# A fused attention kernel: the product for k, its sums of squares and GpSimd's norms one turn sooner

## The reference

```python
q, k, v = x @ Wq, x @ Wk, x @ Wv            # 16 heads of 64
k, v = concat([mem_k, k]), concat([mem_v, v])  # 4 memory rows
q, k = l2norm(q), l2norm(k)                 # per head
dots = einsum('bhid,bhjd->bhij', q, k) * 10
dots = einsum('hg,bgij->bhij', W_pre_th, dots)   # mixes the heads
dots = where(causal, -max, dots)
dots = where(dots < 64th largest of the row, -max, dots)
attn = einsum('hg,bgij->bhij', W_post_th, softmax(dots))
out = (attn @ v) * head_scale * sigmoid(x @ Wg + bg)
return out @ Wo
```

## Time and profile before

| | us |
|---|---|
| median of 3 runs | 2355.67 (2355.18 to 2355.76) |
| the profiled execution | 2356.68 |
| its span, first to last instruction | 2354.8 |
| TensorE busy in it | 2106.7 |
| VectorE busy in it | 1803.1 |
| ScalarE busy in it | 1608.3 |
| GpSimd busy in it | 822.6 |

### The profile page before, as it was taken

How to read it: one execution, slowest core, us unless ns; L and a number is a source line. 1 busy time by engine, 2 the same in 40 slices (tenths; PEclk the granted TensorE clock), 3 DMA queues, 4 the chain that set the end, 5 groups by cost and what they waited for, 6 DMA issues and landing times. The chain is left out here.

```text
span 2354.8 us, 55179 instructions
## 1 busy us (share of the span) xinstructions
PE 2106.7 (89%) x16059; PEld 1369.2 (58%) x16060; DVE 1803.1 (77%) x7282; ACT 1608.3 (68%) x4676; POOL 822.6 (35%) x2274
## 2 busy tenths in 40 slices
PE   7995699999999999999999999999899889985997
PEld 3433456666666666666666666666666666663433
DVE  6565389968996899689958995899589959993446
ACT  4442578857885788688858885888688758861543
POOL 3001444444444443444344434443443344311000
PEclk9996799999999999999999999999999999987998
DMA  5002012111211121012101211121012101212002
GB/s 175 0 0 85 22 40 61 43 25 43 61 43 26 43 61 43 25 43 61 43 25 43 61 43 25 43 61 43 26 43 61 43 23 41 58 38 87 1 0 72
DMA packets 113217, 104.69 MB, mean 44 GB/s; under 512 B 34449, under 2 KB 110865, under 8 KB 112913
## 3 DMA queue, kind: packets, MB, share of 16 engines
q1 hardware_dynamic: 108000, 96.65, 16.1%
q10 hardware_dynamic: 4912, 4.46, 0.6%
HBM read 19.14 MB, written 12.71 MB: 14 GB/s over the span
## 5 line engine op out<-in xcount | busy, mean ns | idle before, releaser
L1052 PE MATMUL bankC<-R,E 128*128 128x128 f32 x2560 | 351.7, 287 | 40.0 <-POOL R L1403 39.9
L1052 PEld LDWEIGHTS bankC<-R,E 128*128 128x128 f32 x2560 | 338.5, 202 | 76.3 <-POOL R L1403 43.9
L1036 PE MATMUL bankB<-raw,mixpre 128*128 128x76 f32 (+37 forms) x1024 | 353.9, 433 | 19.7 <-DMA raw<-SC 19.4
L1252 ACT ACTIVATE S<-bankB,aim_first 128x68 f32<-128x68 f32 (+56 forms) x456 | 232.3, 513 | 163.7 <-PE bankB L1036 163.3
L1499 DVE TENSOR_SCALAR_CACHE_REDUCE S<-S,minus_thr 128x68 f32<-128x68 f32 (+56 forms) x456 | 218.5, 515 | 139.4 <-POOL minus_thr L1396 137.8
L1387 POOL TENSOR_TENSOR S<-S,diagmask 128x8 f32<-128x8 f32 x512 | 106.8, 213 | 522.5 <-ACT S L1252 484.5
L1403 POOL TENSOR_SCALAR R<-mixpost,rinv 128x128 f32<-128x128 f32 x512 | 184.3, 372 | 284.9 <-DVE rinv L1563 284.5
L1559 DVE SCALAR_TENSOR_TENSOR E<-S,limit,E 128x68 f32<-128x68 f32 (+56 forms) x456 | 221.3, 521 | 35.1 <-ACT E L1278 5.2
L1278 ACT ACTIVATE E<-S,nmax 128x12 f32<-128x12 f32 (+56 forms) x512 | 240.0, 528 | 0.7 <-POOL nmax L1417 0.7
L1078 PEld LDWEIGHTS bankM<-PT,V 128*64 128x64 f32 x5120 | 179.0, 138 | 101.4 <-issue 90.9
L1036 PEld LDWEIGHTS bankB<-raw,mixpre 128*128 128x128 f32 x1024 | 159.7, 192 | 120.4 <-issue 82.5
(11 more groups left out here) (177 smaller groups left out, 3935.4 us busy)
## 6 DMA issues: line engine op xcount, KB each, us to landing
X_first<-in_L_attn_x_dram ACTq DMA_DIRECT2D x8, 512.0 KB, 10.4
x<-X_first SPq DMA_DIRECT2D x8, 512.0 KB, 2.9
xt<-x SPq DMA_DIRECT2D x32, 128.0 KB, 2.4
x<-xt SPq DMA_DIRECT2D x32, 128.0 KB, 2.5
X_last<-x SPq DMA_DIRECT2D x8, 512.0 KB, 6.6
out_dram<-X_last SPq DMA_DIRECT2D x8, 512.0 KB, 2.8
raw<-SC SPq DMA_DIRECT2D x8, 258.0 KB, 2.9
raw<-SC SPq DMA_DIRECT2D x8, 254.0 KB, 3.1
```

The costliest lines, as they stand in the source:

```text
L1036: last = nc.tensor.matmul(bankB[n % 2][:, 0:wide(n)], W.mixpre[:, :], raw[n % RAWS][:, 0:wide(n)], start=True, stop=True)
L1052: last = nc.tensor.matmul(bankC[n % 2][:, jb * P:(jb + 1) * P], E[n % EBUFS][:, jb * P:(jb + 1) * P], R[n % RBUFS][:, :], start=True, stop ...
L1252: nc.scalar.activation(S[n % SBUFS][:, 0:wide(n)], src, ACT.Identity, bias=W.aim_first[:, group(n)]).then_inc(S_out, 1)
```

## The change

The product for k, ScalarE's squares and copies of it, stand at g = 2 instead of g = 4, in the second place. Score quarter 1 takes the first place of g = 4, quarter 2 the second. The product for v of tile 1 moves from g = 2 to g = 4. GpSimd's norm of q stands at g = 2 (before: 4), that of k at g = 4 (before: 6). VectorE's sums of k stand at g = 0 (before: 2), in its own count of turns. The list `uses` follows.

```diff
-V1_AT = 2
+V1_AT = 4
...
                 if g == 2:
                     uses += score_steps(2 * t + 1, 0)
+                if g == 2 and ahead:
+                    uses += two("k", t + 1)
+                if g == 4:
+                    uses += score_steps(2 * t + 1, 1)
+                if early_values(t, g):
+                    uses += two("v", t)
                 if g == 4:
                     uses += score_steps(2 * t + 1, 2)
-                if early_values(t, g):
-                    uses += two("v", t)
-                if g == 2:
-                    uses += score_steps(2 * t + 1, 1)
-                if g == 4 and ahead:
-                    uses += two("k", t + 1)
...
                     if g == 4:
-                        score(2 * t + 1, 2)
+                        score(2 * t + 1, 1)
...
-                    if g == 2:
-                        score(2 * t + 1, 1)
-                    if g == 4 and ahead:
+                    if g == 2 and ahead:
                         tokens(t + 1, "k", Wk)
+                    if g == 4:
+                        score(2 * t + 1, 2)
...
-                    if g == 2:
-                        score(2 * t + 1, 1)
-                    if g == 4 and ahead:
+                    if g == 2 and ahead:
                         project_qk(t + 1, 1, "k")
+                    if g == 4:
+                        score(2 * t + 1, 2)
...
                     if g == 2:
                         copy_halo(t + 1)
+                        norm(t + 1, 0)
                     if g == 4:
-                        norm(t + 1, 0)
-                    if g == 6:
                         norm(t + 1, 1)
...
-                if g == 2 and t and t + 1 < NT:
+                if g == 0 and t and t + 1 < NT:
                     squares(t + 1, 1)
```

## The result

The changed kernel takes 2326.05 us (2323.36 to 2327.89), the kernel before beside it 2355.43 us: a ratio of 0.9873 (0.9861 to 0.9884), 29.4 us less where 34.7 were forecast. The profiled span is 2323.6 us, 31.2 less than before.

The account below looks back on a forecast made before the run. Each sequence was taken as bound by TensorE from the R wait to mid tile 1, then by VectorE. Seven sequences at 3.3 us (23) plus 12 in the first gave 35 us: 2321 us, range 2310 to 2332.

Parts of the forecast that it names:

- The wait of kT: TensorE's waits for the transposes of k, 1.12, 2.19 and 1.89 us in tiles 0, 1 and 2, would go.
- The new wait: Tile 0, sequences 2 to 8: ScalarE's k squares wait for VectorE's q sums; TensorE waits 2.3 us, plus 1.4 of clock.
- Clock in tile 1: Slow matmuls behind tile 1's 2.19 us wait cost 1.7 us more; 1.5 us taken as coming back on average.
- Tile 0: Sequences 2 to 8: 1.1 + 0.7 - 2.3 - 1.4 = -1.9 us, a loss.
- Tiles 2 and 3: Tile 2 gains, of 1.9 us, only the 1.5 that VectorE has to give; tile 3 gains 0.
- What TensorE saves beyond that makes the R wait longer (4.2 to about 4.7).: Tile 3: TensorE's further savings only lengthen its R wait at the start of a sequence.
- The move of v: Product for v of tile 1 only changes places with waits: cost 0, bounds 0.5 us either way for a tile.
- The first sequence: k transposes end at about 273.5 instead of 280.5, 7 us; tiles 1 and 2 add 2.2 + 1.7 + 1.4; together 12.
- The sum: 3.3 us a sequence, seven times, 23 us, and 12 in the first sequence: 35 us, predicting 2321 us.
- Covered: Rival: k squares find q sums ready, so ScalarE's new wait is covered; 61 us gain, 2295 us; chance 0.07.
- VectorE bound from tile 1 on: Rival: TensorE's gain comes back as a longer R wait; no change, 2355 us; chance 0.07.
- GpSimd starves VectorE: Rival: thresholds of g = 4 come late behind the q norm in tiles 2 and 3; 2379 us; chance 0.08.

Follow-up runs that it names:

- e1_two_sq: Changed kernel with a squares buffer of its own for k and 5 instead of 6 E buffers: 2290.83 us.
- e9_before_two_sq: Kernel before with a squares buffer of its own for k and five E buffers in place of six: 2343.24 us.
- e12_before_e5: Kernel before with five E buffers in place of six and nothing else: 2345.33 us.
- e2_e5: Changed kernel with 5 instead of 6 E buffers alone: 2325.05 us.
- e3_keep_tile0: Changed kernel, but tile 0 of sequences 2 to 8 keeps the old order of k, quarters, norms and sums: 2307.97 us.
- e8_dve_pad_t2: Changed kernel with one unused sum over 1024 columns (1.2 us) more on VectorE in tile 2 of each sequence: 2335.19 us.
- e7_pe_pad_t2: Changed kernel with 12 more E times R products (2.68 us) on TensorE in tile 2 of each sequence: 2336.63 us.
- e5_k_only: Changed kernel with the product for v of tile 1 back at g = 2, ahead of k: 2323.32 us.
- e4_v_only: Kernel before with the product for v of tile 1 at g = 4 instead of 2 and nothing else: 2343.08 us.

## Why the prediction was right, step by step

*The wait of kT.* Right: 1.12, 2.19 and 1.89 us are gone in all tiles.

*The new wait.* Right in its place, its cause and its number, one a sequence and none in the first; too small in its size, 3.15 us in six of seven where 2.3 was taken and 3 was the upper bound. Where the banks came free was met (20.1 us behind the `R` row before 1399.42, and 1186.7 - 1166.8 = 19.9 in the working); TensorE came there 0.8 us sooner than worked out. e1_two_sq took it away and got 35 us. The clock behind it, 1.4 us, was met: 5.11 against 3.67.

*Clock in tile 1.* Met: -3.7 forecast for the tile, -3.8 measured, and TensorE's busy time there is 1.4 us less a sequence, where 1.5 was booked. Still it is the weakest step, since a wait of 2.19 us doesn't bring the slow clock each time: in sequences 2 to 8 it did six times of seven in the kernel before and in e9_before_two_sq, and four times of seven in e12_before_e5.

*A wait shortened in tile 0.* The 9 us of e12_before_e5 and the 29 of the change overlap. The 9 come mostly from the wait for kT in tile 0, which the change takes away as a whole; on top of the change the same edit gives nothing (e2_e5). The working put the 1.12 us of this wait down to the norm and did not see that the clears of the E buffers stood ahead of it, one of which is worth 0.4 of it.

*Tile 0.* -1.9 forecast, -2.1 measured, by two errors that cancel, which is luck. Idle time was booked as 1.2 us more and rose by 1.9 (the new wait's mean is 3.0). Slow clock was booked as 0.7 more, and TensorE's busy time rose by 0.2: behind the new wait the product for v lost the 1.5 that were said, but other slow stretches of the kernel before went. e3_keep_tile0, 18 us below after, is the price of tile 0 taken back (7 x 2.1 = 15), with tiles 2 and 3 shorter as well.

*Tiles 2 and 3.* "Of 1.9 only the 1.5 that VectorE has" was right in kind: VectorE is the bound, by e8_dve_pad_t2, and e3_keep_tile0 shows its floor, 121.5 to 121.8 us, 1.7 to 2 below before. After is not always on it. Three of its six sequences take 121.6 to 121.8, three 123.1 to 123.4, and in each of the latter VectorE waits again in tile 3, as in this one:

```profile
DVE S L1498 <- POOL minus_thr L1396: 1.5, 2, 1.0
```

These waits start behind a slow stretch of TensorE's. The same mix in a short sequence and in this one, each behind a wait of 1.30 us for `SC`:

```profile
1340.54 1.02 PE L1036 MATMUL bankB<-raw,mixpre 128*128 128x452 f32 x2
...
1570.91 1.87 PE L1036 MATMUL bankB<-raw,mixpre 128*128 128x452 f32 x2
```

The windows of the long stretch and of the short one (length, busy us by engine, granted clock, DMA):

```profile
1488.00:1611.00 123.00, 116.34 (x993) 78.67 (x991) 116.38 (x452) 107.84 (x294) 50.31 (x123) 0.99 0.24 57
```

```profile
1257.00:1379.00 122.00, 115.21 (x994) 77.69 (x992) 116.80 (x455) 107.67 (x294) 49.97 (x125) 1.00 0.25 58
```

TensorE and VectorE are tied there. Cut at the same rows, TensorE is busy 116.2 us in each of the three long sequences and 114.6 in the short ones, for the same work, and that 1.6 tips it. The short ones alone are 1.8 us below before, all six together 1.1, where 1.5 was forecast.

*"What TensorE saves beyond that makes the R wait longer (4.2 to about 4.7)."* Wrong in this kernel. The wait is 4.14 to 4.20 us in sequences 2 to 7 of after, and as long with TensorE padded. In e7_pe_pad_t2 2.68 us more on TensorE lengthen the stretch by 1.5 and don't shorten the wait, so it is no slack of TensorE's. The likely reason, argued and not tested, is that it is the way of the last groups through the other engines, which starts with TensorE's own last mixes. It does not hold its length in every kernel: in e1_two_sq it is 3.55 to 5.72 us, and why is open.

*The move of v, at nothing.* Right in this change (e5_k_only), wrong by itself (e4_v_only, -12 us, all in tile 1: a shorter wait for kT and no slow clock behind it).

*The first sequence.* 12 us forecast, 8.0 measured. From its first mix to that of tile 1 it takes 44.3 us instead of 50.5: 6.2 where 7 was said. Tile 1 gives 3.3. Tiles 2 and 3 take 1.5 more, where 1.4 less was booked. 2.7 us of the difference of the spans lie ahead of attention, where nothing was changed.

*The sum.* First sequence 12 to 8.0; seven sequences 23 to 7 x 2.8 = 20; the opening 2.7 that nobody can claim. In the spans: 10.8 at the first `R` wait (468.32 to 457.54), 16.1 over the next six periods (233.7 to 231.0 us each), 4.3 behind them, together 31.2. The range was given as 2310 to 2332 for gains of 46 to 28 us; 28 us give 2328, so no term stands behind its last 4 us.

*The rivals.* Covered: false in this kernel, but e1_two_sq made it true and gave 2290.8 where that rival had 2295. VectorE bound from tile 1 on: false, its 3.5 us wait in tile 1 shrank to 0.49 (the row at 1245.82), and all its waits for `minus_thr` in that tile 1 from 8.6 to 4.6. GpSimd starves VectorE: false, no wait for `minus_thr` from 1246 to 1379 in the sequence shown, and those of the long sequences stand in tile 3 behind a slow stretch of TensorE's.

## What to carry to other kernels

A step that is moved earlier must be followed to the consumer of its scratch buffer: here one buffer shared by two producers turned 35 us of gain into a wait, more than the 29 that were left, and a second buffer bought them back. When an edit needs a second one "for the room", time the second alone on the kernel before too: here a buffer less was worth 9 us there and nothing after, because it also took a clear of 0.42 us out of the way of a norm that TensorE waited for. And look for the wait next to the place that is worked on: the one for `raw` was in every profile, and putting work there gave 13 us, most of them clock, as a badly placed pad showed by accident.

## What the runs showed of the hardware

Waits of TensorE's between 1 and 2.3 us are often followed by some 1.7 us more for the same matmuls behind them (1.54 and 4.90 us for 1.09 and 3.62). The granted clock is 0.72 from 1256.15 to 1262.30 in the kernel before, so 1.2 GHz for a part of it, and 1.00, 2.4 GHz throughout, for the same matmuls from 1253.75 to 1258.30 in e12_before_e5, behind the same wait of 2.19 us. So it does not follow always. Counted ahead of kT in sequences 2 to 8: of the waits of 2.15 to 2.20 us in tile 1 (before, e9, e12) 16 of 21 were followed by it, of those of 1.55 to 1.64 in tile 1 (e4) none of 7, of those of 1.12 to 1.27 in tile 0 (before, e4) 7 of 14, of those of 0.69 in tile 0 (e9, e12) none of 14. A wait before the edit is thus a poor witness for the clock that the edit will give back.

More work can give back clock: with 2.68 us of products added ahead of the wait for `raw`, TensorE's tile 1 took 51.2 us against 52.4. A piece of work that was needed anyway, moved to the same place, took its tile 1 from 52.5 to 50.8 us at a granted clock of 1.00 in every sequence.
